# First attention of a two-layer model: reciprocals spread by DMA, key halves placed by DMA, values split on GpSimd

## The chip, the cores and the metric

The kernel runs on one NeuronCore of a Trainium2 chip (trn2). A core has TensorE (PE, matrix products), VectorE (DVE), ScalarE (ACT), GpSimd (POOL), SyncE (SP, which here only issues DMAs) and 16 DMA engines. The metric is the device time of one execution in microseconds (us).

## The reference, cut to what matters

Four layers follow each other, each with a residual and a layer norm: attention, a top-2 mixture of experts, a second attention, a second mixture. Only the first attention changes:

```python
# x: (8, 512, 128), 16 heads of 64
w = qkv * (3.0 * x * h * n) ** (-0.25)
q, k, v = jnp.einsum('bsx,xAnh->Abnsh', input, w)
q = q + q_bias[:, None, :]
a = jnp.einsum('bnqh,bnkh->bnqk', q, k) * h ** (-0.5)
a = a + relative_causal(pos_scores)          # from sinusoids and q
a = softmax(where(mask, a, NEG_INF))
o = jnp.einsum('bnqk,bnkh->bqnh', a, v)
out = o.reshape(b, s, n * h) @ out_kernel_scaled + out_bias
x = layernorm(x + out)
```

## The kernel before, in words

Precision near float32 comes from products of float16 halves: an operand is split into a high part (rounded) and a low part (the rest), and three products of halves are summed.

The first attention (`rel_attention_phase`) walks over 8 batches with 8 pairs of heads each: 64 pairs n, with 512 positions. `schedule` gives each engine its own program, a `body` per pair: three pairs written out, a loop of two pairs per turn, and a last one. There is no scheduler; the engines meet by semaphores. For pair n, PE computes the scores of head 0 (`scores(0, n)`) in three PSUM tiles (units u = 0, 1, 2), projects the next pair's keys and queries, multiplies the probabilities of pair n - 2 by the values (`weighted_values`), computes the scores of head 1, projects queries and values, and adds pair n - 2 to the output. DVE takes the row maxima of each unit (`maxima`, L594), ACT the exponentials and their sums (`exps`, L541), one head after the other; the score tiles are shared, so scores of a head wait for the exponentials of the other. ACT then writes the high half of the probabilities (`high`, L550), DVE the low half (`low`, L606, with two SBUF inputs), and SP transposes both by one DMA per head (`turn`, L404), whose result is read two pairs later. DVE also brings queries out of PSUM (`q_evac`, L612) and forms o = product times reciprocal (`normalise`, L619).

Around the change:

- Keys: ACT copies both heads' keys of the next pair to `k32` (`k_copy`, L566). GpSimd splits them head by head straight into `k_h[h]`, `k_l[h]`, tiles of 128 rows of which 64 hold keys and 64 a sinusoid table written once in `setup_phase`. Queries are split between them. One split is three instructions on GpSimd: a one-column gate (L130), the high half (L691), and the low half (L694), which reads two SBUF tiles.
- Values: `project_v` leaves them in `kv_ps`, the PSUM tile that the keys use too. ACT writes the high half (`v_high`, L560), DVE the low half (`v_low`, L623); only then may PE project the next keys.
- Reciprocals: DVE inverts the sums, 4 numbers in each of 128 partitions. The product's rows are dimensions of a head and its columns are positions, so the reciprocals are needed along a row: 16 small float32 matmuls (L466) turn and broadcast them into `r_ps`, and ACT copies that to `r_sb` (`r_copy`, L554).
- Each batch ends with a layer norm: at p == 2 of the next batch DVE sums it (`batch_sum`), at p == 7 it takes the statistics (`batch_stats`), GpSimd the power -0.5 (L137), and DVE applies it (`batch_norm`, L123).
- SP first issues some 36 loads of weights for later layers (L363, L377) in this phase, in program order, and then the transposes.

## Time and profile before

| | us |
|---|---|
| median of 3 runs | 1664.89 (1663.42 to 1665.79) |
| the profiled execution, its own time | 1676.82 |
| its span, first to last instruction | 1675.1 |
| busy PE / DVE / ACT / POOL | 1421.9 / 1262.4 / 971.0 / 879.9 |
| first scores of the first attention start | 42.47 |
| last weighted product of it is normalised | 792.76 |

The profile is one execution. Busy shares are means over stages with different limits; the first attention takes the first 793 us of the span. A busy PE here is one whose matmuls overlap, so it isn't PE at its peak. "SPq" rows are the time that SP takes to issue a DMA; its landing comes later.

### The profile page before, as it was taken

How to read it: one execution, taken by the hardware profiler on the slowest of the kernel's cores; microseconds unless marked ns; L12 is line 12 of the kernel's file. 1: busy time of each engine (PE TensorE's matmuls, PEld its weight loads, DVE VectorE, ACT ScalarE, POOL GpSimd, SP SyncE). 2: the span in 40 equal slices, each digit the busy share in tenths (PEclk: the TensorE clock that was granted, in tenths of full speed). 3: DMA queues.
4: the chain of work that ended last, by engine and by line, in shares of the span. 5: the costliest groups of instructions: out<-in, count | busy, mean ns of one | idle time of the engine just before them, and what ended most of it. 6: DMA issues, size and time to landing. Idle time of an engine off the chain costs nothing. (4 is left out here: it accounts for less than half of the span.)

```text
span 1675.1 us, 38178 instructions
## 1 busy us (share of the span) xinstructions
PE 1421.9 (85%) x12519; PEld 834.2 (50%) x12519; DVE 1262.4 (75%) x2722; ACT 971.0 (58%) x1921; POOL 879.9 (53%) x1203
## 2 busy tenths in 40 slices
PE   4899989898998999897589887489899899898736
PEld 3566666666666666665356555123333333332216
DVE  3788888887888888886688888377787787777534
ACT  2677767676776767675244443156666666665431
POOL 2877778777787777775445555211221221222524
PEclk9899999999999999999699999599999999999977
DMA  5645545454454545544000000411011011010001
GB/s 160 123 113 127 123 98 125 97 122 110 110 125 105 114 111 118 116 110 94 0 2 0 0 0 0 146 48 35 27 39 36 26 39 36 26 40 28 13 12 27
DMA packets 372881, 116.47 MB, mean 70 GB/s; under 512 B 341675, under 2 KB 369312, under 8 KB 372704
## 3 DMA queue, kind: packets, MB, share of 16 engines
q1 hardware_dynamic: 369472, 111.36, 27.9%
q10 hardware_dynamic: 1824, 3.15, 0.6%
q0 software_dynamic: 1536, 1.34, 0.3%
q8 instruction: 27, 0.44, 0.1%
q14 instruction: 22, 0.18, 0.0%
HBM read 20.36 MB, written 12.89 MB: 20 GB/s over the span
## 5 line engine op out<-in xcount | busy, mean ns | idle before, releaser
L541 ACT ACTIVATE prob<-score_ps,nmax 128x512 f32<-128x512 f32 (+3 forms) x512 | 264.9, 526 | 209.0 <-DVE nmax L594 209.0
L1563 DVE TENSOR_REDUCE a_nm<-a_s 128x1 f16<-128x512 f32 x512 | 324.8, 687 | 55.5 <-PE a_s L1335 53.6
L1489 ACT ACTIVATE a_pt<-a_st 128x1024 f32<-128x1024 f32 x256 | 260.4, 1021 | 131.4 <-PE a_st L1353 116.3
L130 POOL TENSOR_TENSOR gate<-mhalf 128x1 f32<-128x1 f32 (+1 forms) x284 | 124.2, 437 | 259.3 <-ACT k L566 137.6
L1335 PE MATMUL a_s<-a_kop,a_qop 128*128 128x512 f16 x512 | 199.6, 391 | 64.2 <-DVE a_nm L1563 47.4
L606 DVE SCALAR_TENSOR_TENSOR p<-prob,p 128x1280 f16<-128x1280 f32 x128 | 204.6, 1598 | 49.8 <-ACT p L550 49.8
L594 DVE TENSOR_REDUCE nmax<-score_ps 128x1 f32<-128x512 f32 (+3 forms) x512 | 213.0, 475 | 3.4 <-PE score_ps L455 3.3
L452 PE MATMUL score_ps<-k_h,q_h 128*128 128x512 f16 (+3 forms) x512 | 158.2, 309 | 22.4 <-ACT prob L541 14.2
L550 ACT ACTIVATE p<-prob 128x1280 f16<-128x1280 f32 x128 | 163.8, 1279 | 6.5
L888 ACT ACTIVATE hid<-fps,b_cols 128x512 f32<-128x512 f32 x130 | 86.3, 687 | 127.2 <-PE fps L848 127.2
L694 POOL TENSOR_TENSOR q_l<-q,q_h 128x512 f16<-128x512 f32 x130 | 152.9, 1176 | 10.8
L454 PE MATMUL score_ps<-k_h,q_l 128*128 128x512 f16 (+3 forms) x512 | 156.9, 306 | 0.0
L453 PE MATMUL score_ps<-k_l,q_h 128*128 128x512 f16 (+3 forms) x512 | 156.7, 306 | 0.0
L694 POOL TENSOR_TENSOR k_l<-k,k_h 64x512 f16<-64x512 f32 x130 | 150.1, 1154 | 10.8
L1353 PE MATMUL a_st<-a_qop,a_kop 128*128 128x512 f16 x512 | 153.4, 383 | 0.2
L984 POOL TENSOR_TENSOR hid_l<-hid,hid_h 128x512 f16<-128x512 f32 x65 | 97.2, 1495 | 107.1 <-DVE hid_h L952 107.1
L1335 PEld LDWEIGHTS a_s<-a_kop,a_qop 128*128 128x128 f16 x512 | 50.8, 99 | 191.0 <-DVE a_nm L1563 156.0
L1366 PE MATMUL a_pv<-a_pt,a_vaug 128*32 128x512 f32 x1024 | 138.3, 612 | 0.7 <-ACT a_pt L1489 0.7
L476 PE MATMUL pv_ps<-pt,v_h 128*64 128x256 f16 (+1 forms) x1536 | 116.9, 256 | 0.3 <-DMA pt<-p 0.3
L455 PE MATMUL score_ps<-causal,ident_bf 128*128 128x128 bf16 x512 | 114.1, 223 | 0.0
L1685 POOL TENSOR_TENSOR a_vaug<-a_v,a_bv 128x128 f32<-128x128 f32 x32 | 14.4, 455 | 185.8 <-PE a_pv L1366 130.9
L862 PE MATMUL fps<-w_h,hid_h 128*128 128x128 f16 (+1 forms) x512 | 93.0, 221 | 21.0 <-POOL hid_l L984 19.4
(331 smaller groups left out, 3433.5 us busy)
## 6 DMA issues: line engine op xcount, KB each, us to landing
a_qop<-q_parts SPq DMA_DIRECT2D x32, 128.0 KB
a_kop<-k_parts SPq DMA_DIRECT2D x128, 24.0 KB
x_tok<-in_L_attn_input_dram SPq DMA_DIRECT2D x4, 512.0 KB, 12.3
pt<-p SPq DMA_TRANSPOSE x128, 4.1
e_w<-in_L_ffn_w_dram SPq DMA_DIRECT2D x1, 2048.0 KB, 8.3
q_parts<-a_q_h SPq DMA_DIRECT2D x16, 128.0 KB
k_parts<-a_k_h SPq DMA_DIRECT2D x16, 128.0 KB
out_dram<-a_res SPq DMA_DIRECT2D x8, 256.0 KB
```

Of the source, the lines that this page charges most:

```text
L452: nc.tensor.matmul(o, q_h[h][:, qs], m.k_h[h][:, 0:w], start=True, stop=False)
L453: nc.tensor.matmul(o, q_h[h][:, qs], m.k_l[h][:, 0:w], start=False, stop=False)
L454: nc.tensor.matmul(o, q_l[h][:, qs], m.k_h[h][:, 0:w], start=False, stop=False)
L541: ins = nc.scalar.activation(prob[h][:, P_OFF[c]:P_OFF[c] + w], score_ps[u][:, col:col + w], ACT.Exp, bias=nmax[h][:, c:c + 1], accum_out= ...
L550: nc.scalar.activation(p16[h][k][:, 0, :], prob[h][:, :], ACT.Copy, scale=P_SCALE).then_inc(p_hi[h], 1)
L594: ins = nc.vector.tensor_reduce(nmax[h][:, c:c + 1], score_ps[u][:, col:col + P * (c + 1)], AX.X, ALU.max, negate=True)
L606: nc.vector.scalar_tensor_tensor(p16[h][k][:, 1, :], prob[h][:, :], P_SCALE, p16[h][k][:, 0, :], ALU.mult, ALU.subtract).then_inc(p_lo[h], 1)
L694: return nc.gpsimd.tensor_tensor(lo, src, hi, ALU.subtract)
L1335: nc.tensor.matmul(s_ps[k][:, :], qop[:, g, c * P:(c + 1) * P], kop[:, hh, g, :], start=True, stop=True).then_inc(s_mm[k], 1)
L1353: mm = nc.tensor.matmul(st_ps[r][:, i, :], kop[:, 2 * r + i, g, kc * P:(kc + 1) * P], qop[:, g, :], start=True, stop=True)
L1489: nc.scalar.activation(pt[kc % 2][r][:, :, :], st_ps[r][:, :, :], ACT.Exp, scale=1.0 / SC).then_inc(exp_done[r], 1)
L1563: nc.vector.tensor_reduce(nm[g % 2][:, c, hh:hh + 1], s_ps[c % 2][:, :], AX.X, ALU.max, negate=True).then_inc(max_done[c % 2], 1)
```

## The change: what it does

- Reciprocals: `rsum` becomes one tile per head; SP stores it to DRAM (`store_r`), and loads it back as 64 equal rows per head (`spread_r`) into `r_bc`, which `normalise` reads with a stride. The 16 matmuls, `r_ps` and ACT's `r_copy` go. `reciprocals(0, n)` moves ahead of `low(0, n)`.
- Keys: one split for both heads into `k16`; two DMAs per pair (`place_k`) copy its halves to `k_hl[h][k]`, now with two buffers per head. PE's scores wait for these DMAs (`k_in`). The setup writes the table to four tiles instead of two, high and low.
- Values: `v_ps` is a PSUM tile of its own; ACT copies it to `v32` after `high(0, n)` (`v_copy`), and GpSimd splits it (`split_v`) after both queries. `v_low` goes from DVE. PE projects values before `weighted_values`.
- Layer norm: `batch_stats` and GpSimd's part move from p == 7 to p == 2; `batch_norm` stays.
- A semaphore of the second layer is merged with another; it changes no order.

```diff
@@ SP
+            def store_r(h, n, k):
+                sp.wait_ge(r_done[h], n + 1)
...
+                sp.dma_start(r_dram[k, h].rearrange("(q c) -> q c", c=QC), rsum[h][k][:, :]).then_inc(r_stored, 16)
+            def spread_r(n, k):
+                sp.wait_ge(r_stored, 32 * (n + 1))
...
+                for h in range(2):
+                    sp.dma_start(r_bc[k][64 * h:64 * h + 64, :], r_dram[k, h:h + 1, :].broadcast_to([64, P * QC])).then_inc(r_in, 16)
+            def place_k(n, k):
+                sp.wait_ge(k_split, n + 1)
...
+                for h in range(2):
+                    r = slice(64 * h, 64 * h + 64)
+                    sp.dma_start(m.k_hl[h][k][r, :, :], k16[r, :, :]).then_inc(k_in, 16)
             def body(n, t, b, p, k):
                 if later(n, 1):
                     turn(1, n - 1, 1 - k)
+                    store_r(1, n - 1, 1 - k)
+                place_k(n + 1, 1 - k)
                 turn(0, n, k)
-            schedule(sp, lambda: None, body, lambda: turn(1, B * PAIRS - 1, 1))
+                if later(n, 1):
+                    spread_r(n - 1, 1 - k)
+                store_r(0, n, k)
+            schedule(sp, lambda: place_k(0, 0), body, last)
@@ PE
                 pe.wait_ge(q_split[h], n + 1)
-                pe.wait_ge(k_split[h], n + 1)
+                pe.wait_ge(k_in, 32 * (n + 1))
@@ weighted_values
-                for c in range(QC):
-                    for h in range(2):
-                        nc.tensor.matmul(r_ps[64 * h:64 * h + 64, c * P:(c + 1) * P], rsum[k][:, c, h:h + 1].to_broadcast([P, 64]),
-                                         m.ident[:, :], start=True, stop=True)
-                pe.wait_ge(v_lo, n + 1)
+                pe.wait_ge(v_split, n + 1)
@@ ACT body
                 high(0, n, t, k)
-                if later(n, 2):
-                    r_copy(n - 2)
+                v_copy(n)
                 exps(1, n, [0, 1, 2])
-                v_high(n, k)
@@ DVE body
-                if behind:
+                if at(p, 2) and not at(b, 0):
                     batch_stats(b - 1)
+                reciprocals(0, n, k)
                 low(0, n, k)
                 if later(n, 2):
-                    normalise(n - 2)
-                reciprocals(0, n, k)
+                    normalise(n - 2, k)
                 maxima(1, n)
                 q_evac(1, n + 1, pw)
-                v_low(n, k)
@@ POOL
             def body(n, t, b, p, k):
-                split_k(0, n + 1)
+                split_k(n + 1)
                 split_q(0, n + 1)
-                split_k(1, n + 1)
                 split_q(1, n + 1)
-                if at(p, PAIRS - 1) and not at(b, 0):
+                split_v(n, k)
+                if at(p, 2) and not at(b, 0):
                     layer_norm_gpsimd(nc, pool, m, b - 1, mv, ve, rstd)
```

On SP at the start of the phase, the end of the loads and what follows, before:

```order
L377 DMA a_bo<-in_L_attn_bo_dram 128x128
L404 DMA_TRANSPOSE pt<-p_00 128x20x128 [waits p_lo0]
L404 DMA_TRANSPOSE pt<-p_10 128x20x128 [waits p_lo1]
L404 DMA_TRANSPOSE pt<-p_01 128x20x128 [waits p_lo0]
L404 DMA_TRANSPOSE pt<-p_11 128x20x128 [waits p_lo1]
```

and of the change (buffers numbered):

```order
L382 DMA a_bo<-in_L1_attn_bo_dram 128x128
L439 DMA k_hl00<-k16 64x1024 [waits k_split]
L439 DMA k_hl10<-k16 64x1024
L439 DMA k_hl01<-k16 64x1024 [waits k_split]
L439 DMA k_hl11<-k16 64x1024
L409 DMA_TRANSPOSE pt00<-p16_00 128x20x128 [waits p_lo0]
L418 DMA r_parts<-rsum00 128x4 [waits r_done0]
```

Behind the last load now come the DMAs that place the keys of the first two pairs, ahead of the first transpose.

On SP in a later pair, before (the transposes of a pair's two heads in turn, nothing else):

```order
L404 DMA_TRANSPOSE pt<-p_10 128x20x128 [waits p_lo1]
L399 REGISTER_ALU
L404 DMA_TRANSPOSE pt<-p_01 128x20x128 [waits p_lo0,pv_mm]
L404 DMA_TRANSPOSE pt<-p_11 128x20x128 [waits p_lo1]
L399 REGISTER_ALU
L404 DMA_TRANSPOSE pt<-p_00 128x20x128 [waits p_lo0,pv_mm]
```

and of the change:

```order
L409 DMA_TRANSPOSE pt<-p_10 128x20x128 [waits p_lo1]
L416 ISA [waits r_done1]
L418 DMA r_parts<-rsum 128x4 [waits r_in]
L432 REGISTER_ALU
L435 REGISTER_ALU [waits k_split]
L439 DMA k_hl<-k 64x1024 [waits s_mm1]
L439 DMA k_hl<-k 64x1024
L404 REGISTER_ALU
L409 DMA_TRANSPOSE pt<-p_01 128x20x128 [waits p_lo0,pv_mm]
L422 REGISTER_ALU
L428 DMA r_bc<-r_parts 64x512 [waits r_stored,o_done]
L428 DMA r_bc<-r_parts 64x512
```

The keys' DMAs stand behind the transpose of head 1 of the pair before and behind the store of its reciprocals.

On GpSimd, the splits of one pair before, ISA and register rows apart:

```order
L130 TENSOR_TENSOR gate<-mhalf 64x1 [waits q_split1,s_mm0,k_out]
L691 AFFINE_SELECT k_h<-k 64x512
L694 TENSOR_TENSOR k_l<-k,k_h 64x512 [waits ra_pool]
L130 TENSOR_TENSOR gate<-mhalf 128x1 [waits k_split0,s_mm0,q_out0]
L691 AFFINE_SELECT q_h<-q_0 128x512
L694 TENSOR_TENSOR q_l<-q_0,q_h 128x512 [waits ra_pool]
L130 TENSOR_TENSOR gate<-mhalf 64x1 [waits q_split0,s_mm1]
L691 AFFINE_SELECT k_h<-k 64x512
L694 TENSOR_TENSOR k_l<-k,k_h 64x512 [waits ra_pool]
L130 TENSOR_TENSOR gate<-mhalf 128x1 [waits k_split1,s_mm1,q_out1]
L691 AFFINE_SELECT q_h<-q_1 128x512
L694 TENSOR_TENSOR q_l<-q_1,q_h 128x512 [waits ra_pool]
```

and of the change:

```order
L131 TENSOR_TENSOR gate<-mhalf 128x1 [waits k_in,k_out]
L712 AFFINE_SELECT k<-k 128x512
L715 TENSOR_TENSOR k<-k 128x512 [waits ra_pool]
L131 TENSOR_TENSOR gate<-mhalf 128x1 [waits s_mm0,q_out0]
L712 AFFINE_SELECT q_h<-q_0 128x512
L715 TENSOR_TENSOR q_l<-q_0,q_h 128x512 [waits ra_pool]
L131 TENSOR_TENSOR gate<-mhalf 128x1 [waits s_mm1,q_out1]
L712 AFFINE_SELECT q_h<-q_1 128x512
L715 TENSOR_TENSOR q_l<-q_1,q_h 128x512 [waits ra_pool]
L131 TENSOR_TENSOR gate<-mhalf 128x1 [waits pv_mm,v_out]
L712 AFFINE_SELECT v_h<-v 128x512
L715 TENSOR_TENSOR v_l<-v,v_h 128x512 [waits ra_pool]
```

There are four splits per pair in both; the third is now the second query's, and the fourth the values'.

## Rows read from the trace of the kernel before

**Rows 1.** One window: length, busy PE, PEld, DVE, ACT, POOL; clock, DMA, GB/s.

```profile
377.76:388.77 11.01, 10.50 (x118) 7.51 (x114) 8.99 (x18) 8.16 (x22) 8.67 (x12) 1.00 0.52 119
```

**Rows 2.** The timeline of DVE over that pair: start, us, what, idle before.

```profile
374.03 0.69 DVE L623 SCALAR_TENSOR_TENSOR v_l<-kv_ps,v_h 128x512 f16<-128x512 f32 x1 [1.05 <-ACT v_h L560]
374.63 1.68 DVE L594 TENSOR_REDUCE nmax<-score_ps 128x1 f32<-128x512 f32 x4
376.31 1.46 DVE L606 SCALAR_TENSOR_TENSOR p<-prob,p 128x1280 f16<-128x1280 f32 x1
...
379.40 1.69 DVE L606 SCALAR_TENSOR_TENSOR p<-prob,p 128x1280 f16<-128x1280 f32 x1 [0.97 <-ACT p L550]
...
381.70 1.65 DVE L594 TENSOR_REDUCE nmax<-score_ps 128x1 f32<-128x512 f32 x4
383.27 0.73 DVE L612 SCALAR_TENSOR_TENSOR q<-q_ps,q_bias,q_mult 128x512 f32<-128x512 f32 x1
```

**Rows 3.** The timeline of ACT over that pair.

```profile
376.93 0.60 ACT L566 ACTIVATE k<-kv_ps 128x512 f32<-128x512 f32 x1
...
378.10 1.27 ACT L550 ACTIVATE p<-prob 128x1280 f16<-128x1280 f32 x1
...
382.39 0.69 ACT L541 ACTIVATE prob<-score_ps,nmax 128x512 f32<-128x512 f32 x1 [2.53 <-DVE nmax L594]
```

**Rows 4.** The timeline of GpSimd over that pair.

```profile
377.76 0.19 POOL L130 TENSOR_TENSOR gate<-mhalf 64x1 f32<-64x1 f32 x1 [1.53 <-ACT k L566]
...
378.59 1.15 POOL L694 TENSOR_TENSOR k_l<-k,k_h 64x512 f16<-64x512 f32 x1
379.91 1.24 POOL L130 TENSOR_TENSOR gate<-mhalf 128x1 f32<-128x1 f32 x1 [0.17 <-POOL k_l L694]
...
383.09 0.19 POOL L130 TENSOR_TENSOR gate<-mhalf 64x1 f32<-64x1 f32 x1
```

**Rows 5.** The timeline of ACT: the values' copies of pairs p = 7, 0, 1, 2.

```profile
313.58 0.61 ACT L560 ACTIVATE v_h<-kv_ps 128x512 f16<-128x512 f32 x1
...
328.83 0.61 ACT L560 ACTIVATE v_h<-kv_ps 128x512 f16<-128x512 f32 x1
...
339.85 0.61 ACT L560 ACTIVATE v_h<-kv_ps 128x512 f16<-128x512 f32 x1
...
351.34 0.61 ACT L560 ACTIVATE v_h<-kv_ps 128x512 f16<-128x512 f32 x1
```

**Rows 6.** The timeline of DVE and GpSimd where a batch is normalised.

```profile
314.83 0.89 DVE L628 TENSOR_TENSOR x_tok<-x_tok,bo_bc 128x512 f32 x1
318.02 1.12 DVE L123 TENSOR_SCALAR x_tok<-ln_y,ln_mv,ln_rstd 128x128 f32 x4 [2.30 <-POOL ln_rstd L137]
...
315.26 1.47 POOL L694 TENSOR_TENSOR q_l<-q,q_h 128x512 f16<-128x512 f32 x1
```

**Rows 7.** The timeline of SP and PE at the start of the first attention.

```profile
60.30 0.43 SPq L377 DMA_DIRECT2D a_bo<-in_L_attn_bo_dram  x1
...
42.47 0.61 PE L452 MATMUL score_ps<-k_h,q_h 128*128 128x512 f16 x1 [1.38 <-POOL q_l L694]
```

**Rows 8.** DMA issues: by line, ns min/median/max; then the page's, us to landing last.

```profile
L404 SPq DMA_TRANSPOSE pt<-p x128: 2296/2554/3421, 60.9 to 785.1; - x128
...
L377 SPq DMA_DIRECT2D a_cols<-in_L_attn_bq_dram x4: 666/666/667, 52.2 to 54.4; - x4
...
tri_ones<-in_c_tri_dram SPq DMA_DIRECT2D x1, 32.0 KB, 1.9
...
c_xe<-slot_rows SPq DMA_DIRECT2D x4, 162.5 KB, 3.8
```

**Rows 9.** The timeline of PE, first unit of a head's scores, first and last matmul.

```profile
301.38 0.39 PE L452 MATMUL score_ps<-k_h,q_h 128*128 128x512 f16 x1
...
302.03 0.22 PE L455 MATMUL score_ps<-causal,ident_bf 128*128 128x128 bf16 x1
```

## What was predicted before the run

> **What bounds the kernel now.** I read the windows of the stages first, then the timelines of one pair engine by engine, then the start of the phase on SP and PE, then the issue times of DMAs. The change touches only the first attention (793 of 1675.1 us) and one piece of setup, so everything is read there. Most pairs take 11.02 us. No engine is full by its own busy time: in such a pair VectorE is busy 8.99, GpSimd 8.67, ScalarE 8.16 [rows 1]. PE's 10.50 counts overlapping matmuls.
>
> The order of time goes in a circle. ScalarE waits 2.53 us for VectorE's maxima before the exponentials of head 1 [rows 3]. VectorE waits 1.05 us for the copy of the high half of the values, and 0.97 us for the high half of head 0's probabilities [rows 2]. Between these waits its work is without a gap.
>
> A second limit lies close by. GpSimd's splits start 2.15 us apart (377.76 to 379.91), but the next one comes 3.18 us later, and its one-column gate takes 1.24 us instead of 0.19: it ends at 381.15, just after VectorE's low half (`low`, 379.40 to 381.09). In turn this `low` takes 1.69 us instead of 1.46, and GpSimd's L694 ended at 379.74, 1.35 us before it [rows 2, 4]. So `low` (two SBUF inputs) and GpSimd's splits take turns. At a batch's end the same is seen with another pair: L694 lasts 1.47 us beside VectorE's bias addition, which ends at 315.72 [rows 6]. One `low` costs GpSimd 1.03 us where it falls on the border of two splits, up to 1.35 inside one. Four splits and two `low` make 4 x 2.15 + 2 x 1.03 = 10.7 us at best and 4 x 2.15 + 2 x 1.35 = 11.3 at worst, beside a pair of 11.02. This limit is nearly reached already, and the change keeps four splits and both `low`.
>
> The Trainium skill says the same of the port ("SBUF — State Buffer", Who interferes with whom): a VectorE instruction with two SBUF inputs and a GpSimd instruction that reads SBUF exclude each other for the whole instruction. By that rule the two waits removed from VectorE give almost nothing; without it a pair would fall to about 10.2 us. The trace's 1.24 us gate agrees with the rule.
>
> **The change, part by part.**
>
> *Start: +21.3 us.* The keys of pair 0 now reach PE through SP, whose program has the loads of later layers first. SP ends the last of them at 60.73, while PE starts the first scores at 42.47 [rows 7]. After it come two issues of 0.43 to 0.67 us (those of the neighbouring loads) and a landing; single DMAs in the trace land 1.9 us, and queued ones 3.8 us, after their issue [rows 7, 8]. 60.73 + 0.3 (setup, below) + 0.5 + 2.2 = 63.7; less 42.47 is 21.3, between 20.9 and 23. Nothing covers it: PE, VectorE and ScalarE have no other work before the first scores, and the rest of the phase hangs on them.
>
> *Setup: +0.3, within the above.* Two more casts and two more subtractions of the table on VectorE, partly in a wait for ScalarE; SP's first load starts when the setup ends.
>
> *Removed from the pairs.* VectorE loses `v_low` (0.69) and the wait of 1.05 before it [rows 2]. ScalarE loses one copy of 0.6 us. PE loses 16 small matmuls, about 1 us of its queue. By the circle alone the next pair's maxima of head 0 could start when PE has the first unit, 1.5 us earlier, and ScalarE would follow 0.7 us earlier: that is the 10.2 us of the next part.
>
> *Added: the keys' path over SP.* Count from the start of head 0's maxima, t. All four reductions end at 1.85, since PE's units come one after another (the first takes 302.25 - 301.38 = 0.87 us [rows 9]). `low` of head 1 then ends at 3.25. Now SP: issuing its transpose takes 2.55 us, the store of reciprocals about 0.55, two placements about 0.5 each, the last landing 1.9 after its issue, with 0.3 for waits [rows 8]: 2.55 + 0.55 + 0.5 + 1.9 + 0.5 = 6.0. PE's first unit and VectorE's start add 1.0. Sum 3.25 + 6.0 + 1.0 = 10.2 us for a pair if nothing blocks. Bounds for the 6.0: 5.5 with the short issues, 8.0 with 0.67 and the landing of 3.8. I take 6.0, since the nearest row is the lone DMA.
>
> *Added: the values' split on GpSimd.* It follows the second query's split, which needs `q_evac` of head 1. From t: high half ready 4.77 later (374.63 to 379.40), `low`, `normalise` and the start of maxima 2.3, maxima 1.57, `q_evac` 0.73 [rows 2], in all 9.4. Two splits from 9.5 end at 13.8, which is 13.8 - P in the next pair, P being its length. There `low` of head 1 wants to start at 1.85 and has to wait for L694: it ends at 13.8 - P + 1.4. Then P = (15.2 - P) + 6.0 + 1.0, so P = 11.1. GpSimd's own sum gives 10.7 to 11.3. The two couple, and each collision costs a little of both; I take P = 11.2, range 10.7 to 11.6. Over 63 steps: 63 x (11.2 - 11.02) = +11.3 us, between -20 and +37.
>
> The keys' copy is ready 2.9 after t (376.93 + 0.60 - 374.63, rows 2, 3), before GpSimd is free, so this wait isn't late. SP issues two transposes (5.1) and six further DMAs (about 3.2) in a pair, 8.3 of 11.2, so it isn't full; behind the placement waits only the transpose of head 0, which is read two pairs later. The reciprocals' way back starts behind that transpose, some 9 us after t, and is needed a pair later, some 17 us after t. Its strided read I cost at nothing, 0 to 0.2 us per pair, covered by VectorE's new slack of some 2 us.
>
> *Batch ends: -17.5 us.* The pair that holds the norm takes 15.25 us, and p == 2 takes 11.49, together 4.70 over two plain ones [rows 5]. Of it, 2.30 is VectorE's wait for GpSimd's power, the rest bias and norm [rows 6]. The result is now there five pairs earlier, so the wait goes, and bias (0.8) and norm (1.05) fall partly in VectorE's slack. They leave about 0.8. At p == 2 the statistics (1.2) fall in VectorE's slack too, but GpSimd's part (about 1.3) stands in a full queue: 1.4 left. So 4.70 - 2.2 = 2.5 each, seven times 17.5; between 7 (all of it on the path) and 26.
>
> *End: 0.* The last store and spread take two DMA times, beside a transpose and a product of the same length, and one copy of 0.6 goes: -0.5 to +2.
>
> Sum: 21.3 + 11.3 - 17.5 + 0.3 = +15.4 us. The profiled execution took 1676.82 us, so a profile of the changed kernel would show 1692. It lies 11.9 above the median of the runs; the same difference on the median gives 1664.9 + 15.4, about 1680 us.
>
> [...]
>
> **The rivals.**
>
> *A: the pairs get shorter by more than the start costs.* If both `low` fall on borders of splits (1.03 each), P is 10.7; with 26 saved at batch ends the sum is 21.3 - 20 - 26 = -25, 1640 us. For it: in this trace head 0's `low` does fall on a border, and PE and ScalarE have room. Against: the border is met because GpSimd has idle time there, and it will have none. It decides from P below about 10.95, where the sum is zero with the 17.5.
>
> *B: the keys land late.* With 3.8 in place of 1.9 and slow issues the path is 8.0; then P = (15.2 + 9.0)/2 = 12.1, above which the value split no longer blocks. Taking half of it, P = 11.7: 21.3 + 43 - 17.5 = +47, 1712 us. For it: every placement follows a transpose on the same queue. Against: the transpose lands before the placement is issued.
>
> *C: the start costs nothing.* Were SP's loads out of the way (shorter without a profiler, or placement issued before), the sum is 1664.9 - 6 = 1659. Against: SP's order of rows shows the placement behind all loads.
>
> **How the numbers follow.** What can be told from no change is about 0.2%, 3.3 us. The forecast (slower by 5 to 30 us, 1670 to 1695) gets 0.53; A 0.26, B 0.15, C 0.06. Slower by over 0.2%: 0.51 of the forecast, all of B, 0.01 of A: 0.67. The same: 0.02 of the forecast, 0.05 of A, 0.01 of C: 0.08. Faster: 0.20 of A, 0.05 of C: 0.25. The likeliest case gives 1680. Its own range is 1670 to 1695. For 8 in 10 it reaches into A, down to 1650, and into B, up to 1712.
>
> **What would show it.** The first scores start at about 63.7 in the profile; if they start before 50, the start term is wrong. The seven long pairs shrink from 15.25 to about 12, and VectorE's wait for the power is gone. In plain pairs GpSimd has under 0.5 us of idle time, and head 1's `low` or GpSimd's L131 is stretched to over 1.7 and 1.2 us. Head 0's scores wait for the keys' DMA. If plain pairs are under 10.9 us with GpSimd idle, the coupling is wrong; if over 11.6, the placement's landing was mis-sized.

## The result, and the profile after

The changed kernel takes 1715.55 us (median of 4 runs, 1714.14 to 1717.61), the kernel before 1665.29 beside it: ratio 1.0304 (95% interval 1.029 to 1.0319), 50.3 us slower. The forecast was 1680, its own range 1670 to 1695, the one for 8 in 10 1650 to 1712. The profiled execution took 1714.84, its span 1712.8, so it is a typical one; that of before lay 11.9 above its median, and the two profiles differ by 38 us only. Inside the first attention they differ by more: the last weighted product is normalised at 847.6 instead of 792.76, 54.8 later. What follows the first attention, which the change leaves alone, takes 865.2 us in the changed kernel's profile and 882.3 in that of before. This difference goes with the chip: the kernel before takes 1676.5 to 1676.8 us (medians) beside e1 to e8, e13 and e14, and 1665.2 to 1665.6 beside e9 to e12 and e15, and in the profiles of the first group the rest takes 878 to 885 us, in those of the second 865 to 868 (e14 apart).

Windows of both kernels in the middle of the phase (length; busy PE, PEld, DVE, ACT, POOL; granted clock; DMA; GB/s), before first:

```profile
400.00:600.00 200.00, 182.65 (x1953) 128.44 (x1949) 162.95 (x316) 138.02 (x356) 152.54 (x209) 1.00 0.49 111
```

```profile
400.00:600.00 200.00, 167.97 (x1571) 114.68 (x1572) 158.04 (x273) 128.25 (x324) 155.04 (x203) 0.92 0.65 152
```

The numbers in brackets count instructions. Every engine but GpSimd does less in the same time; PE's granted clock falls from 1.00 to 0.92 of full speed, and the DMA share rises by a third. No engine is busy all the time: what grew is waiting.

The start, which answers to [rows 7]: SP and then PE, timeline.

```profile
59.94 0.43 SPq L382 DMA_DIRECT2D a_bo<-in_L_attn_bo_dram  x1
60.50 12.71 SPq L439 DMA_DIRECT2D k_hl<-k  x4
...
64.24 0.58 PE L498 MATMUL score_ps<-k_hl,q_h 128*128 128x512 f16 x1 [23.77 <-DMA k_hl<-k]
```

First scores at 64.24 instead of 42.47: +21.8 us. SP's last load starts at 59.94, 0.36 us earlier than before, so the 0.3 us expected from the setup are not there.

The pairs, which answer to [rows 1 to 4]. A pair's length is the time from ACT's copy of the keys in it to the next one. A plain pair is any but the third of a batch (p == 2) and the last (p == 7, the long one, which holds the norm). Before, the 36 plain pairs of batches 3 to 8 take 11.01 to 11.16 us each; now 10.6 to 14.1, in the mean 11.87. They are not alike: the fourth pair of a batch (p == 3), which follows GpSimd's part of the norm, takes 13.36 in the mean of the six, the other thirty 11.57. Two neighbours are shown (13.32 us, then 10.78), then GpSimd, DVE and SP.

```profile
501.65 0.59 ACT L599 ACTIVATE k<-k_ps 128x512 f32<-128x512 f32 x1
...
514.97 0.59 ACT L599 ACTIVATE k<-k_ps 128x512 f32<-128x512 f32 x1
...
525.75 0.59 ACT L599 ACTIVATE k<-k_ps 128x512 f32<-128x512 f32 x1
```

```profile
504.19 2.45 POOL L715 TENSOR_TENSOR k<-k 128x512 f16<-128x512 f32 x1
...
516.57 1.16 POOL L715 TENSOR_TENSOR k<-k 128x512 f16<-128x512 f32 x1
...
525.19 2.42 POOL L715 TENSOR_TENSOR v_l<-v,v_h 128x512 f16<-128x512 f32 x1
...
528.41 2.31 POOL L715 TENSOR_TENSOR k<-k 128x512 f16<-128x512 f32 x1
```

```profile
501.04 2.46 DVE L631 SCALAR_TENSOR_TENSOR p<-prob,p 128x1280 f16<-128x1280 f32 x1
...
504.16 1.46 DVE L631 SCALAR_TENSOR_TENSOR p<-prob,p 128x1280 f16<-128x1280 f32 x1
...
511.77 0.69 DVE L619 TENSOR_REDUCE nmax<-score_ps 128x1 f32<-128x512 f32 x1 [2.92 <-PE score_ps L501]
...
525.13 1.46 DVE L631 SCALAR_TENSOR_TENSOR p<-prob,p 128x1280 f16<-128x1280 f32 x1
...
528.21 1.49 DVE L631 SCALAR_TENSOR_TENSOR p<-prob,p 128x1280 f16<-128x1280 f32 x1 [0.87 <-ACT p L589]
```

```profile
503.60 2.52 SPq L409 DMA_TRANSPOSE pt<-p  x1
...
507.08 1.14 SPq L439 DMA_DIRECT2D k_hl<-k  x2
```

At 504.16 DVE's low half starts, and GpSimd's subtraction of the keys, issued 0.03 us later, takes 2.45 us instead of 1.16: it stands until 505.6. In the next pair it falls in a gap (516.57) and the pair is short. Then, at 525.19, the values' subtraction meets head 1's low half, and the keys' one at 528.41 meets head 0's. They are placed at 530.96. It goes the other way as well: the `low` at 501.04 took 2.46 us. From 100 to 760 us, 13 of 55 keys' subtractions, 4 of 55 of the values and 23 of 110 `low` take over 2 us; alone they take 1.16 and 1.46.

The fourth pair is long in another way. One of 13.81 us (from the copy at 392.32 to that at 406.14), GpSimd, then DVE:

```profile
392.78 1.45 POOL L137 TENSOR_TENSOR ln_ve<-ln_mv,ln_eps 128x4 f32<-128x4 f32 x1
...
395.28 1.06 POOL L131 TENSOR_TENSOR gate<-mhalf 128x1 f32<-128x1 f32 x1
...
396.98 1.15 POOL L715 TENSOR_TENSOR k<-k 128x512 f16<-128x512 f32 x1
```

```profile
394.83 1.45 DVE L631 SCALAR_TENSOR_TENSOR p<-prob,p 128x1280 f16<-128x1280 f32 x1
...
402.94 0.69 DVE L619 TENSOR_REDUCE nmax<-score_ps 128x1 f32<-128x512 f32 x1 [3.41 <-PE score_ps L501]
```

The keys' subtraction isn't stretched. It is late: GpSimd first has the values' split and the norm's two operations, 2.5 us in all, and then its gate stands behind `low` until 396.3. The keys of the next pair are split at 398.1, and VectorE waits 3.41 us for their scores. Of the seven fourth pairs behind a norm five take 13.4 to 14.1 us and two 10.9; that of the first batch, where no norm is due, takes 10.70.

PE and its clock at the late keys: first and last matmul of the unit after a wait of 2.27 us, the first after one of 0.97, then windows around the former.

```profile
510.17 0.61 PE L498 MATMUL score_ps<-k_hl,q_h 128*128 128x512 f16 x1 [2.27 <-DMA k_hl<-k]
...
511.42 0.31 PE L501 MATMUL score_ps<-causal,ident_bf 128*128 128x128 bf16 x1
...
522.36 0.39 PE L498 MATMUL score_ps<-k_hl,q_h 128*128 128x512 f16 x1 [0.97 <-DMA k_hl<-k]
```

```profile
508.00:510.00 2.00, 0.00 (x0) 0.00 (x0) 0.86 (x2) 1.97 (x8) 1.57 (x4) 1.00 0.73 169
510.00:512.00 2.00, 1.83 (x6) 0.84 (x7) 0.23 (x1) 0.68 (x1) 1.92 (x4) 0.53 1.27 287
```

PE did nothing for two microseconds, and in the next two the granted clock was 0.53, about the lower of its two levels (1.2 GHz, the other is 2.4). The unit then takes 1.56 us (510.17 to 511.73) where [rows 9] show 0.87. After the wait of 0.97 the first matmul took 0.39, as in [rows 9].

The leading waits from 100 to 760 us (total, times, longest):

```profile
ACT prob L580 <- DVE nmax L619: 217.5, 99, 4.1
DVE nmax L619 <- PE score_ps L501: 94.2, 63, 3.5
PE score_ps L498 <- DMA k_hl<-k: 73.2, 45, 3.3
POOL gate L131 <- ACT k L599: 61.7, 45, 3.8
POOL gate L131 <- DVE q L637: 60.2, 50, 1.5
```

The last two are GpSimd's: over some 55 pairs it stands idle 121.9 us, 2.2 us a pair, waiting for the keys' copy and for VectorE's queries.

The batch's end, which answers to [rows 5, 6]:

```profile
351.89 2.83 DVE L124 TENSOR_SCALAR x_tok<-ln_y,ln_mv,ln_rstd 128x128 f32 x4
```

The wait of 2.30 for GpSimd's power is gone, but here the norm takes 2.83 us instead of 1.12, beside GpSimd's splits. The long pairs shrink from 15.24 to 13.05 in the mean. The third pairs of batches 2 to 8 grow from 11.50 to 12.29, and the fourth pairs, behind GpSimd's part of the norm, from 11.03 to 13.01.

### The profile page after: what moved, and what is told of

Its sections match the earlier page's. It is cut to its first block and busy times, and to the rows that moved or that the text cites. A ratio compares the mean times of both kernels' runs of the same rounds, so it can differ in the third digit from the quotient of the medians.

```text
span 1712.8 us, 37091 instructions
## 1 busy us (share of the span) xinstructions
PE 1376.8 (80%) x11495; PEld 790.1 (46%) x11495; DVE 1284.8 (75%) x2662; ACT 951.5 (56%) x1857; POOL 915.3 (53%) x1201
## 5 line engine op out<-in xcount | busy, mean ns | idle before, releaser
L1514 ACT ACTIVATE a_pt<-a_st 128x1024 f32<-128x1024 f32 x256 | 260.5, 1021 | 121.9 <-PE a_st L1378 118.8
L619 DVE TENSOR_REDUCE nmax<-score_ps 128x1 f32<-128x512 f32 (+3 forms) x512 | 221.7, 484 | 139.6 <-PE score_ps L501 136.6
L131 POOL TENSOR_TENSOR gate<-mhalf 128x1 f32<-128x1 f32 x283 | 138.8, 490 | 280.8 <-ACT k L599 121.4
L498 PE MATMUL score_ps<-k_hl,q_h 128*128 128x512 f16 (+3 forms) x512 | 165.9, 324 | 124.3 <-DMA k_hl<-k 112.6
L631 DVE SCALAR_TENSOR_TENSOR p<-prob,p 128x1280 f16<-128x1280 f32 x128 | 221.2, 1728 | 29.0 <-ACT p L589 28.8
L500 PE MATMUL score_ps<-k_hl,q_l 128*128 128x512 f16 (+3 forms) x512 | 166.2, 325 | 0.0
L499 PE MATMUL score_ps<-k_hl,q_h 128*128 128x512 f16 (+3 forms) x512 | 165.8, 324 | 0.0
L715 POOL TENSOR_TENSOR q_l<-q,q_h 128x512 f16<-128x512 f32 x130 | 150.3, 1156 | 10.8
L498 PEld LDWEIGHTS score_ps<-k_hl,q_h 128*128 128x128 f16 x512 | 53.1, 104 | 171.3 <-DMA k_hl<-k 51.3
L501 PE MATMUL score_ps<-causal,ident_bf 128*128 128x128 bf16 x512 | 119.1, 233 | 0.0
```

What stands on the lines that cost most here:

```text
L498: nc.tensor.matmul(o, q_h[h][:, qs], m.k_hl[h][k][:, 0, 0:w], start=True, stop=False)
L499: nc.tensor.matmul(o, q_h[h][:, qs], m.k_hl[h][k][:, 1, 0:w], start=False, stop=False)
L500: nc.tensor.matmul(o, q_l[h][:, qs], m.k_hl[h][k][:, 0, 0:w], start=False, stop=False)
L619: ins = nc.vector.tensor_reduce(nmax[h][:, c:c + 1], score_ps[u][:, col:col + P * (c + 1)], AX.X, ALU.max, negate=True)
L631: nc.vector.scalar_tensor_tensor(p16[h][k][:, 1, :], prob[h][:, :], P_SCALE, p16[h][k][:, 0, :], ALU.mult, ALU.subtract).then_inc(p_lo[h], 1)
L715: return nc.gpsimd.tensor_tensor(lo, src, hi, ALU.subtract)
```

## The sum, by the trace

From the copies of the keys, 63 steps take 12.01 us in the mean instead of 11.48, +33.4 in all. By kind (the seventh long pair lies behind the last copy):

| pairs | before | changed | sum |
|---|---|---|---|
| long, 6 | 15.24 | 13.05 | -13.2 |
| third of a batch, 7 | 11.50 | 12.29 | +5.5 |
| fourth of a batch, 7 | 11.03 | 13.01 | +13.9 |
| the others, 43 | 11.03 | 11.66 | +27.1 |

With the start 21.8 + 33.4 = 55.2, against 54.8 at the last normalisation. The medians differ by 50.3; the profile of the changed kernel taken again (e12) has 843.9 there, 51.1 more than before, so single executions of it differ by some us in this phase.

## The experiments

Ratios are to the kernel before, run on the same chip; 3 rounds, intervals of some +-0.0017. Each kernel is the changed one with the edit shown, unless it says otherwise. Lengths of plain pairs are means over the 36 of batches 3 to 8 in the profile; fourth pairs are among them.

**e1: the loads ahead of the phase**

```diff
@@ SP
+(setup block, behind the loads of x)  36 loads of later weights
-(first attention, ahead of place_k(0)) 36 loads of later weights
```

> The changed kernel, with the 36 loads of later layers issued by SP in the setup, behind the loads of x, instead of at the start of the first attention. Theory (start gap): PE's first scores wait for the keys' placement behind these loads (64.24 us against 42.47 before); without them they start at about 43, and the time falls by 20 to 22 us, to about 1694. Rival (the gap is given back, or the loads are in the way of the setup's own loads): less than 10 us are won, and the setup ends later than 36 us.

Measured 1.0191 (1.0174 to 1.0208), 19 us less than the change. First scores at 48.83, 15.4 us earlier than in the change: SP issues loads in setup until 41.03, and the first placement starts at 45.75, against 40.46 in e8. So 15 of the 19 us are the start; the rest is in the pairs (11.92 us in the mean for 12.01).

**e2: reciprocals read in a row**

```diff
-                 r_bc[k][:, :].rearrange("p (q c) -> p c q", c=QC), ALU.mult)
+                 r_bc[k][:, :].rearrange("p (c q) -> p c q", q=P), ALU.mult)
```

> The changed kernel, but the normalisation reads the spread reciprocals in a row instead of with a stride of four (the kernel leaves out the right order of the reciprocals). Theory (the strided read costs 0.39 us per pair and stands between low half and maxima of head 1): the instruction falls from 1.07 to 0.68 us, the time by 15 to 25 us. Rival (VectorE now has slack, 2.9 us before some maxima, that hides it): by 0 to 4 us.

(This kernel leaves out the right order of the reciprocals.) 1.0295 (1.0278 to 1.0312): nothing, though the normalisation fell from 1.07 to 0.68 us. Plain pairs 11.71.

**e3: keys placed ahead of head 1's transpose**

```diff
+                place_k(n + 1, 1 - k)
                 if later(n, 1):
                     turn(1, n - 1, 1 - k)
                     store_r(1, n - 1, 1 - k)
-                place_k(n + 1, 1 - k)
```

> The changed kernel, with the placement of the keys put ahead of head 1's transpose and store in SP's program of a pair. Theory (the keys' way over SP ends last: transpose issue 2.55, store 0.4, then placement): the wait of PE's scores for the keys shrinks by about half and the time falls by 10 to 20 us. Rival (GpSimd's key split, held up by the low halves, ends last): the keys come no earlier, 0 to 5 us either way. Where SP's wait for the split delays head 1's transpose too much: slower by some us.

1.0290 (1.0272 to 1.0307): nothing. Plain pairs 11.75, still between 10.6 and 14.2.

**e4: values split by ScalarE and VectorE again**

```diff
@@ ACT v_copy
-                nc.scalar.activation(v32[:, :], v_ps[:, :], ACT.Copy, scale=W_SCALE)
+                nc.scalar.activation(v_h[k], v_ps[:, :], ACT.Copy, scale=W_SCALE)
@@ DVE body, after q_evac(1, n + 1, pw)
+                v_low(n, k)
@@ POOL body
-                split_v(n, k)
```

> The changed kernel, with the values' split back on ScalarE (high half, where it now copies them) and VectorE (low half, 0.69 us, behind the query of head 1), in their own PSUM tile; GpSimd keeps three splits a pair. Theory (GpSimd and the low halves exclude each other, 8.6 + 2.7 us are the bound of a pair): a pair loses a split of 2.15 us, and the time falls by 15 to 30 us. Rival (the keys' way over SP bounds): 0 to 5 us, with GpSimd idle longer. A third: VectorE's added 0.69 is on the path, up to +10.

1.0061 (1.0044 to 1.0077), 2.4% or 41 us less: more than the whole loss beyond the start. Plain pairs 11.06, the fourth ones 10.81. VectorE does 0.69 us more per pair and the kernel is faster; GpSimd's keys subtraction is back at 1.16 us, and none of it nor of `low` takes over 2 us. What of it is GpSimd's time and what is the meeting with `low`, the next three tell.

**e5: values between the queries on GpSimd**

```diff
                 split_k(n + 1)
                 split_q(0, n + 1)
+                split_v(n, k)
                 split_q(1, n + 1)
-                split_v(n, k)
```

> The changed kernel with one move on GpSimd: the values are split between head 0's and head 1's queries, in the place where GpSimd stood idle 1.48 us a pair for VectorE's head 1 queries. Theory (the values' split delays the next keys' split, with it the placement and the scores): the keys are free 1.5 us earlier in most pairs, ratio to the kernel before 1.012 to 1.021 (from 1.030), the scores' wait for the placement of the keys falls from 82+51 us to under 90 in all. Rival (GpSimd's work is all on one path and it only trades keys for queries): head 1's queries come 1.9 us late, head 1's scores wait for them instead, ratio 1.028 to 1.045.

1.0104 (1.0087 to 1.0121), a little beyond the theory. All the work is kept; only its place changed, into the stretch in which GpSimd waited for VectorE's queries, and none of the three subtractions, keys', values' and `low`, takes over 2 us any more (groups of instructions, 100 to 760 us):

```profile
L715 POOL TENSOR_TENSOR k<-k 128x512 f16<-128x512 f32 x58 | 67.2, 1159 | 4.8
L715 POOL TENSOR_TENSOR v_l<-v,v_h 128x512 f16<-128x512 f32 x58 | 67.0, 1156 | 4.8
...
L631 DVE SCALAR_TENSOR_TENSOR p<-prob,p 128x1280 f16<-128x1280 f32 x116 | 178.8, 1542 | 43.2 <-ACT p L589 43.2
```

(busy us, mean ns, idle before; in the changed kernel the means over the same stretch are 1458, 1245 and 1721). Plain pairs 11.07, the fourth ones 10.80. The two engines still hold each other up, but at the one-column gate in front of a split: its mean is 541 ns here and 520 in the change, alone it takes 190.

**e6: e4 with fills in the place of the values' split**

```diff
@@ e4, POOL body
+                for i in range(4):
+                    nc.gpsimd.memset(v32[:, S * i:S * i + S], 0.0)
```

> The kernel of e4 (values split by ScalarE and VectorE as before) with four fills of 128x512 f32 on GpSimd in the place where the changed kernel splits the values: about the same 1.9 to 2.1 us of GpSimd's time, but nothing that reads SBUF. The output is unchanged; only a spare tile is written. Theory 1 (what costs is the time in GpSimd's queue before the next keys' split): the ratio goes back from 1.006 to 1.020 to 1.030. Theory 2 (what costs is that the values' split and VectorE's low halves hold each other up at SBUF): the ratio stays at 1.004 to 1.011, and the low halves stay unstretched beside the fills.

1.0179 (1.0162 to 1.0196), 20 us more than e4. Neither theory alone. The pairs tell where: the long pair goes from 12.79 to 14.35 us (7 times, 11 us of the 20), the fourth from 10.81 to 11.96, and the other plain ones not at all (11.11, then 11.05). So two microseconds more on GpSimd cost an ordinary pair nothing. In the long pair it is the norm that grows, by 1.54 us: DVE in e4, then DVE and GpSimd in e6.

```profile
431.71 1.95 DVE L124 TENSOR_SCALAR x_tok<-ln_y,ln_mv,ln_rstd 128x128 f32 x4
```

```profile
437.59 3.49 DVE L124 TENSOR_SCALAR x_tok<-ln_y,ln_mv,ln_rstd 128x128 f32 x4
...
438.77 1.92 POOL L755 MEMSET v<- 128x512 f32 x4
```

The fills read nothing from SBUF, and the norm is held beside them all the same. In the fourth pair the keys' subtraction comes right behind the fills and GpSimd's part of the norm, and meets `low` in each of the seven batches that have a norm there:

```profile
384.78 1.01 POOL L138 TENSOR_TENSOR ln_rstd<-ln_ve,mhalf 128x4 f32<-128x4 f32 x1
...
386.60 2.28 POOL L723 TENSOR_TENSOR k<-k 128x512 f16<-128x512 f32 x1
```

In the first batch, which has none, the fourth pair takes 10.67.

**e9: e6 with a split of a spare tile instead of the fills**

```diff
@@ e6, POOL body
-                for i in range(4): memset(v32[:, S * i:S * i + S])
+                split(slice(0, P), v32[:, :], spare[:, 0, :], spare[:, 1, :], 4 * n + 8)
```

> The kernel of e6 with the four fills replaced by a split of a spare tile that never changes (a filter into 16 bits of 0.61 us and a subtraction with two operands from SBUF of 1.16 us): slightly less of GpSimd's time than the fills' 2.11 us, at the same place, with no data that anything waits for. The output is unchanged. Theory (GpSimd's two-operand subtraction and VectorE's low halves can't run beside each other; which comes first changes from pair to pair, and when the keys' subtraction loses, the scores wait): the plain pairs become irregular again (between 10.7 and 14 us, mean over 11.3), the subtraction of the keys goes from 1.28 to over 1.4 us in the mean, ratio 1.024 to 1.036. Rival (only GpSimd's time counts): plain pairs stay at 10.8 to 10.9, ratio 1.012 to 1.018, no more than with the fills (1.018).

1.0375 (1.0348 to 1.0401), worse than the change itself (e12, on the same chip: 1.0304; the two intervals just touch), with less of GpSimd's time than the fills and no data that anything waits for. GpSimd and DVE of e6 (100 to 760 us), then of e9 (100 to 740):

```profile
L755 POOL MEMSET v<- 128x512 f32 x228 | 109.6, 527 | 0.0
L723 POOL TENSOR_TENSOR k<-k 128x512 f16<-128x512 f32 x56 | 72.0, 1285 | 4.7
...
L633 DVE SCALAR_TENSOR_TENSOR p<-prob,p 128x1280 f16<-128x1280 f32 x113 | 173.8, 1538 | 41.5 <-ACT p L589 41.5
```

```profile
L724 POOL TENSOR_TENSOR k<-k 128x512 f16<-128x512 f32 x53 | 74.8, 1411 | 4.4
L724 POOL TENSOR_TENSOR spare<-v,spare 128x512 f16<-128x512 f32 x53 | 69.9, 1319 | 4.4
...
L634 DVE SCALAR_TENSOR_TENSOR p<-prob,p 128x1280 f16<-128x1280 f32 x106 | 180.2, 1700 | 28.4 <-ACT p L590 28.2
```

With writes in that place `low` takes 1.54 us, as in e4, with reads 1.70. Plain pairs go from 11.20 to 11.76, and from 6 above 11.6 us to 16 of 36; the long pair stays at 14.34. So the exclusion between two readers costs 2.0% (e6 to e9). The Trainium skill says it so ("SBUF — State Buffer", Who interferes with whom): a VectorE instruction with two SBUF inputs contends with a GpSimd instruction that reads SBUF, not with one that only writes it. These two runs agree for `low`, with 1700 and 1538 ns.

The 1.2% from e4 to e6 is not plain time of GpSimd. It comes from two other meetings, of the norm with the fills and of the keys' subtraction with `low`, and the norm's part doesn't carry over to the change, whose long pair takes 13.05.

**e7: the kernel before with the norm's statistics early, alone**

```diff
@@ before, DVE and POOL body
-                if behind:
+                if at(p, 2) and not at(b, 0):
                     batch_stats(b - 1)
-                if at(p, PAIRS - 1) and not at(b, 0):
+                if at(p, 2) and not at(b, 0):
                     layer_norm_gpsimd(nc, pool, m, b - 1, mv, ve, rstd)
```

> The kernel before with one part of the change alone: the layer norm's statistics on VectorE and the two small operations on GpSimd in the third pair of the next batch instead of its last. My term: minus 17.5 us of the whole (7 to 26), ratio 0.9895 (0.984 to 0.996); the pair at the end of a batch falls from 15.25 us to about 12.7. Rival: the third pair, which then has the sum over the batch and the statistics both, grows by as much (ratio 0.998 to 1.002).

0.9961 (0.9946 to 0.9975): 6.5 us, a third of my term. The third pair takes 11.53 and the fourth 10.83, so here GpSimd's part costs nothing. The wait is gone, but bias and norm now run beside GpSimd's splits, and long pairs fall to 14.6 only (timeline of DVE and GpSimd; [rows 6] show 0.89, 1.12 and the wait):

```profile
405.94 1.29 DVE L628 TENSOR_TENSOR x_tok<-x_tok,bo_bc 128x512 f32 x1
407.15 2.52 DVE L123 TENSOR_SCALAR x_tok<-ln_y,ln_mv,ln_rstd 128x128 f32 x4
...
406.85 0.43 POOL L130 TENSOR_TENSOR gate<-mhalf 128x1 f32<-128x1 f32 x1 [0.17 <-POOL k_l L694]
```

**e8: e4 with most loads in setup, the last 14 behind the first placement**

```diff
@@ e4, SP
+(setup block, behind the loads of x) 22 loads of later weights
+            def first():
+                place_k(0, 0)
+                rest()          # 14 loads of columns and biases, 8.7 us of issue
```

> The kernel of e4 and most of the second attention's loads issued during setup, the last 12 or so (8.5 us of issue) after the first placement of the keys, so that the first keys are placed as soon as they are split. Theory (the start costs 21.8 us, and the rest of e4 is otherwise near the kernel before): first scores at 43 to 45 us, ratio 0.992 to 0.996, faster than the kernel before. Rival (the first transposes of the probabilities are now late behind the loads and the gain of the start is lost again): 1.000 to 1.006.

0.9935 (0.9918 to 0.9951). First scores at 43.51, 20.5 us earlier than in e4, and 21 us less in time: the start term nearly whole.

**e10: e5 with e8's loads**

```diff
@@ e5, SP
+            loads as in e8
```

> The changed kernel with two moves and nothing undone: the values split between the queries of head 0 and of head 1 (e5), and most loads in setup with the rest behind the first placement (e8). If the two gains add, as the one falls on the pairs and the other before the first pair: 1.0104 minus 0.0126, ratio 0.998 (0.995 to 1.001). Rival (the start's gain is absorbed where the pipeline fills): 1.003 to 1.010.

0.9944 (0.9922 to 0.9966): the two gains add, and 0.4% more, just beyond the range, which no run explains. So the change, with nothing of it undone, is 0.6% faster than the kernel before once two orders are put right.

**e11: e8 with e3's order on SP**

```diff
@@ e8, SP body
+                place_k(n + 1, 1 - k)   # ahead of turn(1, ...), as in e3
```

> The kernel of e8 with the placement of the keys ahead of head 1's transpose in SP's queue. Theory (in the pairs at a batch's start, 11.5 to 13.5 us in e8, the placement waits behind a transpose of 2.5 us): ratio 0.988 to 0.992 (from 0.9935). Rival (as in e3, SP's order is not what ends last): 0.9925 to 0.995.

0.9789 (0.9772 to 0.9806): both theories were wrong by size. The same edit that gave nothing in e3 gives 1.5% here. Plain pairs 10.82, most of them 10.64, the fourth ones 11.06, and among the ten longest waits none is for the placement.

**e12: the changed kernel again**

```diff
(no edit)
```

> The changed kernel itself on the chip of these runs, to compare e9 and e10 with it directly. Ratio 1.029 to 1.032, as before.

1.0304 (1.026 to 1.0349), on the chip of e9 to e11. Plain pairs 11.80, the fourth ones 13.11 over batches 3 to 8, 10.87 in the first batch, which has no norm there.

**e13: e10 with e3's order on SP**

```diff
@@ e10, SP body
+                place_k(n + 1, 1 - k)   # ahead of turn(1, ...)
```

> The kernel of e10 (everything of the change kept, GpSimd still splits the values) with the placement of the keys ahead of head 1's transpose. Theory (in the changed kernel the order on SP was worth nothing, e3, because the keys were already late behind GpSimd's stretched subtraction; without that, the placement is the last, as in e11): ratio 0.978 to 0.984 (from 0.9944), plain pairs at 10.65 us. Rival (in e11 it is the missing split on GpSimd that let the placement pay): 0.990 to 0.996.

0.9873 (0.9856 to 0.9890): between the two ranges, 0.7% better than e10, half of what e11 won. So the late keys did hide the order's cost, but with the values on GpSimd only half is to be had. Most pairs fall to 10.64 us as in e11; the fourth takes 12.20 for 11.06 and the long one 13.12 for 12.79. In the fourth the keys' subtraction meets `low` (its mean, 1159 ns in e10; 6 of 59 take over 2 us):

```profile
L729 POOL TENSOR_TENSOR k<-k 128x512 f16<-128x512 f32 x57 | 73.8, 1295 | 4.8
```

**e14: e13 with the reciprocals stored in the order of reading**

```diff
-                sp.dma_start(r_dram[k, h].rearrange("(q c) -> q c", c=QC), rsum[h][k][:, :])
+                sp.dma_start(r_dram[k, h].rearrange("(c q) -> q c", q=P), rsum[h][k][:, :])
```

> The kernel of e13 with the reciprocals stored in the order in which the normalisation reads them, so that VectorE reads them contiguously (0.68 for 1.07 us), for a store of single numbers of 4 bytes with a step instead of 16 bytes in a row. Theory (VectorE bounds the plain pairs now, with no wait for the scores left): 0.39 us a pair, ratio 0.010 to 0.015 less than e13's. Rival (the store now takes longer than the time it has, or VectorE still has other slack): within 0.003 of e13, or slower.

1.3146 (1.3124 to 1.3168), 527 us slower. The store is 512 numbers of 4 bytes instead of 128 rows of 16. Queue lines (packets, MB, share of 16 engines) of e13 and of e14, then the latter's DMA issues, us to landing last:

```profile
q1 hardware_dynamic: 408544, 145.46, 37.1%
```

```profile
q1 hardware_dynamic: 457696, 145.46, 74.8%
...
k_hl<-k SPq DMA_DIRECT2D x130, 128.0 KB, 7.4
...
pt<-p SPq DMA_TRANSPOSE x128, 8.2
```

The 49,152 packets more (128 stores x 384) take 0.748 x 2204.3 - 0.371 x 1653.1 = 1036 us of all 16 engines; as an estimate that puts all of it on them, 0.34 us of one engine each. Placements land after 7.4 us instead of the change's 2.4, transposes after 8.2 instead of 4.2.

**e15: e11 with the reciprocals read in a row**

```diff
@@ e11, DVE normalise: as in e2
```

> The kernel of e11 (ratio 0.9789) with the normalisation reading the reciprocals contiguously as they lie, in the wrong order, so that its output is wrong in the normalisation; all else is the same. It takes the strided read away without touching the store, which e14 could not. Theory (VectorE, which waits for the scores only 5.7 us in 58 pairs of e11, now bounds the plain pairs, so that the 0.39 us come off each): plain pairs 10.25, ratio 0.964 to 0.971. Rival (a chain between the engines, with VectorE's 0.9 us of waits a pair for ScalarE's high half in it, bounds them): plain pairs stay at 10.6, ratio 0.976 to 0.980.

(This kernel, too, leaves out the right order of the reciprocals.) 0.9644 (0.9627 to 0.9660), 1.45% less than e11. Plain pairs 10.39, most 10.25. The normalisation in e11, then here:

```profile
L661 DVE TENSOR_TENSOR o<-pv_ps,r_bc 128x512 f32<-128x512 f32 x54 | 57.2, 1059 | 2.0 <-DMA r_bc<-r_parts 1.0 <-issue 0.9
```

```profile
L661 DVE TENSOR_TENSOR o<-pv_ps,r_bc 128x512 f32<-128x512 f32 x57 | 38.7, 679 | 1.8 <-DMA r_bc<-r_parts 1.6
```

The 0.38 us that nobody paid for in e2 come off each pair here. No run has both the read in a row and the right order at this price; e14, which has both, pays for them in the store.

## Why the prediction was wrong

The sum was +15.4 us, and the trace has 55.2. Of the 40 us between them, 24 lie around the batch's end and 16 in the other pairs.

*Start, +21.3:* right (21.8), and shown by e8, which takes nearly all of it away. The 21.3 already held the 0.3 of the setup, which the sum then adds again; the trace has no such delay (59.94 for 60.30).

*The pair, P = 11.2:* this step failed. "GpSimd's own sum gives 10.7 to 11.3. The two couple, and each collision costs a little of both; I take P = 11.2." The 43 pairs away from the batch's end take 11.66, +27.1 us instead of +11.3 for all 63. I had the right two parties and the right instruction, but took the coupling for a steady state with a small price, on a GpSimd without idle time ("under 0.5 us"). It has 2.2 us a pair. The price is in the meetings: where the keys' subtraction falls just behind the start of `low` it loses 1.3 us, the keys go out later by that, the scores and with them the next `low` move, and the next meeting differs. There is no cover, because all of it lies on one chain: `low`, GpSimd, SP, placement, scores, maxima. Two more sizes on that chain were low. The way over SP, 6.0, is 6.6 us in the pair shown (503.60 to 510.17). And PE's first unit, 0.87, takes 1.56 after a wait at the lower clock; I had not priced the clock at all. e4 and e5 show that without the long meetings most of the pairs' loss is gone (those 43 take 11.22 and 11.24 us), and e6 and e9 that it takes a reader to bring it back; the part of the clock is read from the trace and was not tried by itself.

My first use of the Trainium skill's rule on two readers ("SBUF — State Buffer", Who interferes with whom) was to cost the removal of VectorE's waits at nothing, which was right in the changed kernel. Where I used it for a sum of times, I should have used it for an order: which of two readers comes 0.03 us first decides 1.3 us.

*Batch ends, -17.5:* this step failed too, and is the larger part of the miss. The long pairs give 13.2 us, the third and fourth take 19.4 back, so the sum is +6.2; done alone the move gives 6.5 (e7). Two errors are in it. I let the wait of 2.30 go and added nothing for what it had kept apart: the norm then runs beside the splits and takes 2.5 to 2.9 us instead of 1.1. That sentence, "bias (0.8) and norm (1.05) fall partly in VectorE's slack", was wrong in kind. And I took GpSimd's part for 1.4 us in the third pair. With the values' split ahead of it, it mostly makes the next keys late, and the fourth pair takes 13.0 us. The same part at the same place costs nothing in the fourth pair when the values are split elsewhere (10.8 in e4, e5 and e7). That it is this part and not a chance meeting is read from the traces: in the first batch, without it, the fourth pair takes 10.70 (10.87 in e12, but 12.42 in e3). No run moved it alone out of the changed kernel.

*Strided read, 0 to 0.2:* right for this kernel (e2), for the reason given. It holds only while VectorE waits for scores: in e15 it is 0.43 us a pair (10.82, then 10.39).

*Removed work, nothing gained from it:* right in the changed kernel. With the orders mended it does pay: in e13, which keeps the whole change, most pairs take 10.64 us where before they took 11.02.

*The rivals:* B had nearly the time (1712) with the wrong cause. It wanted a landing of 3.8 us; the median is 2.4 (3.8 the longest), and e3 shows that the transpose ahead of the placement cost nothing as things stood. A's condition, both `low` on borders of splits, is nearly what e5 brings about by hand: most pairs then take 10.8 (A had 10.7), but with the start still in it e5 is 1% slower than before, and the 26 us at the batch ends are not there. Without the start e10 is faster. C's condition, loads out of the way, is met in e8 and was worth its 21 us.

## What to carry to other kernels

Where two engines exclude each other and both lie on one loop-carried chain, don't add up their times: look at which instruction comes just ahead of which, and move work into a stretch where the other engine is idle or reads PSUM. A removed wait may have kept two such instructions apart. Filler that only writes is no neutral stand-in for work that reads: it held the norm (e6). And an edit that gives nothing (e2, e3) may only be hidden: each was worth 1.5% once what ended last was gone. A mean over equal pairs hides which of them is long; look at each place of the loop by itself.

## What was not expected of the hardware

- The same instruction of VectorE with one wide SBUF input, the norm (`x_tok<-ln_y`, 4 times), takes 1.12 us alone, 1.95 to 3.39 beside GpSimd's splits (2.83 to 2.87 in the changed kernel), and 3.49 beside a split and fills. I had looked for the exclusion only at instructions with two. The Trainium skill ("SBUF — State Buffer", Who interferes with whom) lists `tensor_scalar` among those that can take both port pairs in a two-port mode; the times beside the splits agree with it, and which mode ran no trace shows.
- Stores of single 4-byte numbers cost, by the estimate at e14, 0.34 us of a DMA engine each, and what is issued beside them on SP's queue lands late (7.4 us for 2.4).
- A read with a step of 16 bytes makes the normalisation 1.06 us for 0.68. The Trainium skill ("SBUF — State Buffer", Door 1) says that SBUF has lines of 16 bytes and that each access that crosses into a new one pays a penalty. It gives no size, and the trace can't show the cause.
